# Where each tile's first expert weights come from: loads by SyncE into four slots in place of VectorE copies

## What is computed

```python
z = _layernorm(x, ln_g, ln_b)
logits = jnp.einsum('bth,he->bte', z, rW) + rb
probs = jax.nn.softmax(logits, axis=-1)
topv, topi = jax.lax.top_k(probs, TOP_K)
...
hid = jax.nn.gelu(jnp.einsum('bth,ehf->btef', z, W1) + b1, approximate=False)
outs = jnp.einsum('btef,efh->bteh', hid, W2) + b2
mixed = jnp.sum(outs * w[..., None], axis=2)
return x + mixed
```

## Time and profile before

| what | us |
|---|---|
| median of 3 runs (lowest, highest) | 833.07 (832.11, 835.7) |
| the profiled execution | 831.73 |
| its span in the trace | 829.9 |
| PE busy in it | 753.3 (91%) |
| DVE, ACT, POOL busy | 631.3, 563.3, 535.9 |
| granted TensorE clock, mean | 0.956 |

### The profile page before, as it was taken

One profiled execution on the slowest core, in us unless ns is written; L12 is line 12 of the kernel. 1 busy time (PEld: TensorE's weight loads), 2 busy tenths in 40 slices (PEclk: granted clock), 3 DMA queues, 4 the chain that ended last, 5 costly groups with the idle time before them and its releaser, 6 DMA issues.

```text
span 829.9 us, 26089 instructions
## 1 busy us (share of the span) xinstructions
PE 753.3 (91%) x8080; PEld 587.1 (71%) x8081; DVE 631.3 (76%) x1781; ACT 563.3 (68%) x1469; POOL 535.9 (65%) x609
## 2 busy tenths in 40 slices
PE   7888989999999999999999997666967898999995
PEld 4555666777777777777777665455867797999995
DVE  7788998988999999989999999963347763444442
ACT  3466777878888888878888874445464554666663
POOL 5433757777777767768767765354555556777773
PEclk9999999999999999999999999757989898999998
DMA  8566775777687786886786775551333333443432
GB/s 213 149 145 154 153 159 121 166 169 162 154 190 154 162 182 140 182 162 156 170 175 155 176 148 103 147 168 39 60 56 53 52 46 58 77 61 62 62 64 27
DMA packets 154004, 104.46 MB, mean 126 GB/s; under 512 B 68365, under 2 KB 149561, under 8 KB 153817
## 3 DMA queue, kind: packets, MB, share of 16 engines
q1 hardware_dynamic: 135502, 79.47, 43.7%
q0 software_dynamic: 10944, 14.10, 10.8%
q10 hardware_dynamic: 7498, 10.18, 4.2%
HBM read 36.65 MB, written 17.33 MB: 65 GB/s over the span
## 4 chain that ended last, share of the span: by engine, by line
PE 59%; DVE 13%; DMA 10%; POOL 5%; issue 5%; SPq 3%; ACT 2%; DVEq 1%; ACTq 0%; POOLq 0%
PE s_row L1021 9%; PE pj L916 8%; PE zt L962 7%; PE s_row L930 7%; PE s_t L950 7%; PE pj L883 7%; PE pj L1032 4%; PE zt L1032 4%; DVE negmax L1409 3%; DMA stack_x<-in_x 2%; DMA out_x<-index_space,idx_s 2%; PE pj L901 2%; SPq L672 2%; DMA stack_x<-k_part 2%; PE pj L1009 1%
## 5 line engine op out<-in xcount | busy, mean ns | idle before, releaser
L1409 DVE TENSOR_REDUCE negmax<-s_row 100x1 f32<-100x361 f32 x512 | 251.0, 522 | 20.0 <-PE s_row L930 16.0
L1226 ACT ACTIVATE p_t<-s_t 128x400 f32<-128x400 f32 x384 | 187.9, 499 | 89.7 <-PE s_t L950 82.1
L930 PE MATMUL s_row<-stack_x,q_stack 125*128 125x361 bf16 x512 | 134.0, 321 | 22.8 <-DVE negmax L1409 16.3
L744 POOL DMA_INDIRECT out_x<-index_space,idx_s x56 | 91.3, 1631 | 74.6 <-DMA out_x<-index_space,idx_s 27.8
L950 PE MATMUL s_t<-q_stack,stack_x 128*128 128x100 bf16 x1536 | 129.1, 212 | 8.8 <-ACT p_t L1226 6.1
L950 PEld LDWEIGHTS s_t<-q_stack,stack_x 128*128 128x128 bf16 x1536 | 94.6, 99 | 53.1 <-issue 25.0
L1021 PE MATMUL s_row<-w_qkv,v_aug 128*128 128x128 f32 x912 | 119.1, 288 | 8.2 <-DVE v_aug L1504 8.2
L1021 PEld LDWEIGHTS s_row<-w_qkv,v_aug 128*128 128x128 f32 x912 | 114.0, 204 | 9.5 <-DVE v_aug L1504 9.4
L1414 DVE TENSOR_SCALAR p_t<-p_t 128x1200 f32<-128x1200 f32 x128 | 100.8, 787 | 11.1 <-ACT p_t L1226 11.0
L916 PE MATMUL pj<-w_qkv,ct 128*128 128x256 f32 x384 | 104.9, 396 | 0.3 <-ACT k_rest L1147 0.3
L962 PE MATMUL zt<-p_t,v_aug 128*32 128x100 f32 (+1 forms) x3072 | 96.1, 260 | 0.0
(11 more groups left out here) (247 smaller groups left out, 1436.6 us busy)
## 6 DMA issues: line engine op xcount, KB each, us to landing
stack_x<-k_part SPq DMA_DIRECT2D x192, 192.0 KB, 3.6
q_stack<-q_part SPq DMA_DIRECT2D x192, 64.0 KB, 2.0
ct<-in_ctx_t SPq DMA_DIRECT2D x32, 361.0 KB, 4.4
stack_x<-in_w ACTq DMA_DIRECT2D x8, 512.0 KB, 6.2
w_s<-in_w ACTq DMA_DIRECT2D x14, 256.0 KB, 3.1
zscr<-zn SPq DMA_DIRECT2D x32, 100.0 KB
z_in<-zscr SPq DMA_DIRECT2D x32, 100.0 KB
zf_d<-zf_s SPq DMA_DIRECT2D x32, 100.0 KB
```

Source lines behind the costliest of these rows:

```text
L744: pool.indirect_dma_start(out_rows[0:n], bass.IndirectOffsetOnAxis(idx_out(k), 0), result_rows(k), None, bounds_check=n - 1, oob_is_err=Fa ...
L930: nc.tensor.matmul(s_row[h % 2][:, 0:KEYS], q_stack[0:MROW, b.slot, h, :], k_stack[0:MROW, b.slot, h, 0:KEYS], start=True, stop=True).then ...
L1226: nc.scalar.activation(p_t[:, quad % 2, kt, :], s_t[g % 2][:, 0:4 * Q], ACT.Exp).then_inc(exp_done, 1)
L1409: v.tensor_reduce(negmax[:, b.slot, h:h + 1], s_row[h % 2][0:Q, 0:KEYS], AXIS.X, ALU.max, negate=True).then_inc(max_done, 1)
```

## The change

The host packs each expert's first weights and bias into one DRAM block of 128 rows of 1028 floats (4112 bytes a row, 526 KB). `w1_s`, `b1_s`, their loads and the DVE step `weights` go. Four slots `w1_k` take their place; SP reads the expert of tile k+4 from `te_i`, waits until `gelu(k)` has read its slot, and loads the block. `up` waits for that DMA, `gelu` takes its bias from the slot. The first four loads stand at a place of their own ("w1", 375). `gating` gets a wait for `gated` of four tiles before. The places of routing, early tiles and the last three batches are all dealt anew; of these tables only a part is shown.

```diff
-        w1_s = sb(es, "w1_s", [128, 2, E, HF])
+        w1_k = sb(es, "w1_k", [128, 4, 2 * HF + 4])
...
-            w1_k = [v_aug[:, k].rearrange("p n w -> p (n w)")[:, 0:2 * HF] for k in (2, 0)]
...
-                    sp.dma_start(b1_s[:], b1).then_inc(b1_loaded, 16)
+
+                def load_w1(k):
+                    sp.wait_ge(tiles_known, 2 if k.known and k.index >= NF else 1)
+                    e = sp.value_load(te_i[0:1, bass.ds(k.index, 1)], min_val=0, max_val=E - 1)
+                    after(sp, gelu_done, 4 * (k.index - 3))
+                    sp.dma_start(w1_k[:, k.ring], w1[bass.ds(e, 1)].rearrange("e p f -> p (e f)")).then_inc(w1_copied[k.ring], 16)
+
+                def tile_step(k):
+                    if not k.known or k.index + 4 < NT:
+                        load_w1(k.later(4))
...
+                        if at("w1"):
+                            for c in range(4):
+                                load_w1(Tile(0, c))
+                        for k in tiles_at(turn, i, s):
+                            tile_step(k)
...
+                remaining(sp, tile_step, LOOP[0])
...
-                    pe.wait_ge(w1_copied, k.index + 1)
+                    pe.wait_ge(w1_copied[k.ring], 16 * k.turn + 16)
...
-                    act.wait_ge(b1_ready, k.index + 1)
...
-                                             bias=b1_k[:, k.slot, j:j + 1]).then_inc(gelu_done, 1)
+                                             bias=w1_k[:, k.ring, 2 * HF + j:2 * HF + j + 1]).then_inc(gelu_done, 1)
...
+                    after(dve, y_ready, k.index - 3)
...
-                def weights(k):
-                    e = dve.value_load(te_i[0:1, bass.ds(k.index, 1)], min_val=0, max_val=E - 1)
-                    after(dve, up_done, k.index - 1)
-                    v.tensor_scalar(w1_k[k.slot].rearrange("p (c f) -> p c f", c=2), w1_s[:, :, bass.ds(e, 1), :].rearrange("p c e f -> p c (e f)"),
-                                    1.0, None, ALU.mult).then_inc(w1_copied, 1)
...
-TILE_PLACE = [393, 393, 394, 396, 396, 400, 406, 406, 407, 410, 412, 412, 415, 415, 421, 425, 427, 438, 440, 442, 442, 446, 448, 451]
-WEIGHT_LOADS = (27, 30, 31)
+TILE_PLACE = [392, 393, 395, 395, 395, 398, 403, 406, 408, 409, 410, 411, 417, 417, 422, 422, 423, 423, 429, 434, 434, 435, 436, 439]
+WEIGHT_LOADS = (30, 31)
```

More of the change, by code:

```diff
@@ L155, in pipeline, with build @@
         iteration(0, i)
-def build(nc, x, ctx_t, wq_t, bq, wk_t, bk, wv_t, bv, gamma, beta, ln_g, ln_b, rw, rb, w1, b1, w2, b2,
+def build(nc, x, ctx_t, wq_t, bq, wk_t, bk, wv_t, bv, gamma, beta, ln_g, ln_b, rw, rb, w1, w2, b2,
           ident_d, route_c, zscr, zf_d, out):
@@ L182, in build @@
         lnb_c = sb(es, "lnb_c", [128, 2])
-        b1_s = sb(es, "b1_s", [128, E, 4])
-        route_const, rw_scaled, shift_done, rb_shifted, b1_loaded = (sem(k) for k in (
-            "route_const", "rw_scaled", "shift_done", "rb_shifted", "b1_loaded"))
+        route_const, rw_scaled, shift_done, rb_shifted = (sem(k) for k in ("route_const", "rw_scaled", "shift_done", "rb_shifted"))
         rb_s = sb(es, "rb_s", [Q, E])
-        w1_s = sb(es, "w1_s", [128, 2, E, HF])
+        w1_k = sb(es, "w1_k", [128, 4, 2 * HF + 4])
         ident = sb(es, "ident", [128, 128])
@@ L195, in build @@
         ident_ready = sem("ident_ready")
-        w1_loaded = sem("w1_loaded")
+        w1_copied = [sem(f"w1_copied{k}") for k in range(4)]
         x2_step = sem("x2_step")
@@ L558, in build @@
             gate = sb(att, "gate", [128, 4])
-            b1_k = sb(att, "b1_k", [128, 2, 4])
             idx_g_ready, idx_s_ready = sem("idx_g_ready"), sem("idx_s_ready")
@@ L562, in build @@
             scattered = [sem(f"scattered{k}") for k in range(2)]
-            zgt_done, zgt_copied, up_done, b1_ready, gelu_done = (sem(k) for k in ("zgt_done", "zgt_copied", "up_done", "b1_ready", "gelu_done"))
+            zgt_done, zgt_copied, up_done, gelu_done = (sem(k) for k in ("zgt_done", "zgt_copied", "up_done", "gelu_done"))
             gate_ready, y_biased, down_done, y_ready = (sem(k) for k in ("gate_ready", "y_biased", "down_done", "y_ready"))
-            w1_copied = sem("w1_copied")
             N_W2 = 16 * (E + 1)
@@ L1250, in iteration @@
                             queries_high(a)
[L1251 to L1255, removed]
                         n, g = lagging(turn, i, s, SCORES_LAG)
@@ L1521, in tile_step @@
                     if not k.known or k.index + 2 < NT:
-                        weights(k.later(2))
                         gating(k.later(2))
@@ L1531, in first_tiles @@
                     dve.wait_ge(w2_loaded, N_W2)
[L1532 to L1536, removed]
                     for c in range(2):
@@ L1675 @@
 PLACE = {"PE": PE_PLACE, "ACT": ACT_PLACE, "DVE": DVE_PLACE, "POOL": POOL_PLACE, "SP": SP_PLACE}
-ROUTE_PLACE = {"sum_const": 295, "ask0": 299, "exp0": 309, "prob0": 311, "choose00": 321, "choose01": 335, "sum0": 353, "ends0": 354, "places0": 357,
[6 rows of a table removed]
-TILE_PLACE = [393, 393, 394, 396, 396, 400, 406, 406, 407, 410, 412, 412, 415, 415, 421, 425, 427, 438, 440, 442, 442, 446, 448, 451]
-WEIGHT_LOADS = (27, 30, 31)
-TAIL = {29: {'PE': {'z': 8, 'zft': 2, 'router': 4}, 'ACT': {'td': 7, 'u': 6, 'y': 14, 'zft': 2, 'zt': 6}, 'DVE': {'z': 9, 'stats': 3, 'var': 4, 'stats2': 8, 'var2': 10, 'logits': 2}, 'POOL': {'u': 2, 'rstd': 2, 'xb': 7, 'y': 10, 'rstd2': 11}, 'SP': {'zout': 5, 'zin': 8, 'zf': -1}},
-        30: {'PE': {'z': 10, 'zft': -7, 'router': -6}, 'ACT': {'td': 12, 'u': 3, 'y': 5, 'zft': -6, 'zt': 4}, 'DVE': {'z': 7, 'stats': 0, 'var': 1, 'stats2': 3, 'var2': 4, 'logits': -6}, 'POOL': {'u': 1, 'rstd': 2, 'xb': 2, 'y': 4, 'rstd2': 5}, 'SP': {'zout': 5, 'zin': 11, 'zf': 0}},
-        31: {'PE': {'z': 9, 'zft': -6, 'router': -5}, 'ACT': {'td': 7, 'u': 4, 'y': 5, 'zft': -7, 'zt': 6}, 'DVE': {'z': 7, 'stats': 0, 'var': 3, 'stats2': 3, 'var2': 4, 'logits': -6}, 'POOL': {'u': 0, 'rstd': 1, 'xb': -3, 'y': 3, 'rstd2': 4}, 'SP': {'zout': 8, 'zin': 10, 'zf': -10}}}
@@ new lines @@
+ROUTE_PLACE = {"sum_const": 304, "ask0": 307, "exp0": 309, "prob0": 311, "choose00": 322, "choose01": 335, "sum0": 350, "ends0": 351, "places0": 357,
+               "taken0": 361, "split0": 368, "hot00": 369, "hot01": 370, "number00": 371, "number01": 373, "query00": 374, "query01": 374, "lanes00": 373,
+               "lanes01": 374, "lanes02": 375, "lanes03": 376, "gates0": 345, "store0": 348, "picks0": 378, "experts0": 377, "w1": 375, "index0": 379,
+               "gather": 380, "rows": 385, "affine": 383, "tiles": 386, "gelu": 386, "ask1": 402, "exp1": 400, "prob1": 405, "choose10": 406,
+               "choose11": 409, "sum1": 409, "gates1": 409, "store1": 417, "ends1": 411, "places1": 415, "taken1": 415, "split1": 418, "hot10": 419,
+               "hot11": 419, "hot12": 423, "hot13": 424, "query10": 418, "query11": 423, "query12": 423, "query13": 424, "lanes10": 423, "lanes11": 428,
+               "experts1": 429, "picks1": 434, "index1": 432}
@@ new lines @@
+TILE_PLACE = [392, 393, 395, 395, 395, 398, 403, 406, 408, 409, 410, 411, 417, 417, 422, 422, 423, 423, 429, 434, 434, 435, 436, 439]
+WEIGHT_LOADS = (30, 31)
+TAIL = {29: {'PE': {'z': 9, 'zft': 2, 'router': 3}, 'ACT': {'td': 9, 'u': 6, 'y': 14, 'zft': 4, 'zt': 7}, 'DVE': {'z': 9, 'stats': 3, 'var': 4, 'stats2': 10, 'var2': 11, 'logits': 3}, 'POOL': {'u': 1, 'rstd': 2, 'xb': 0, 'y': 4, 'rstd2': 10}, 'SP': {'zout': 6, 'zin': 9, 'zf': 1}},
+        30: {'PE': {'z': 7, 'zft': -8, 'router': -6}, 'ACT': {'td': 12, 'u': 3, 'y': 5, 'zft': -6, 'zt': 7}, 'DVE': {'z': 7, 'stats': 0, 'var': 1, 'stats2': 3, 'var2': 4, 'logits': -5}, 'POOL': {'u': 2, 'rstd': 2, 'xb': 2, 'y': 3, 'rstd2': 6}, 'SP': {'zout': 4, 'zin': 12, 'zf': -4}},
+        31: {'PE': {'z': 7, 'zft': -9, 'router': -6}, 'ACT': {'td': 8, 'u': 2, 'y': 4, 'zft': -8, 'zt': 7}, 'DVE': {'z': 8, 'stats': -1, 'var': 0, 'stats2': 1, 'var2': 3, 'logits': -7}, 'POOL': {'u': -1, 'rstd': 1, 'xb': -3, 'y': 2, 'rstd2': 2}, 'SP': {'zout': 6, 'zin': 7, 'zf': -11}}}
```

8 lines of the change are left out of this document (2 added, 6 removed), and 6 rows, old and new, of the table ROUTE_PLACE.

## The result

The changed kernel takes 852.47 us (median of 4 runs, 851.41 to 853.22) against 832.99: **1.0225 times as long, 95% interval 1.0194 to 1.0256**. The forecast was 825.6 in a range of 812 to 843.

A forecast was written before the change was run, and what follows sets the result against it. PE was taken as full in attention and late tiles, with gains only between about 552 and 690, where it waits; -8.0 - 5.0 + 5.5 = -7.5 gave 824.2 us profiled, 825.6 median, range 812 to 843.

The forecast's parts named there:

- The copy: Last batches to early tiles: without DVE's copy of first weights, PE's waits and the slow clock behind them go; 8.0 us won.
- the late routing: Dealt anew between tile steps: one more DVE stretch holding a result up, 1.6 us taken off the copy's gain.
- The loads: 57 loads of 526 KB, one per tile, fit the DMA engines but delay scatters and gathers: 5.5 us lost.
- L: What the loads add to the landing of a scatter or gather: 0.75 us, between 0 and 2.3.
- the slack of 0.63 a group: Late tiles: POOL's 14.33 us beside PE's 14.96 per four-tile group leaves 0.63 us for L; eight groups cost 1.0.
- The first gathers: First gather, beside the first four loads, and tile 24's gather: each later by L, together 1.5 us.
- The new places: Last batches and early tiles: tile 5 ahead of batch 31's rows wins 3.7 us, an earlier wait 1.3; together 5.0.
- At nothing: Costed at zero: removed ACT issues, SP's new waits for expert list and gelu, DVE's gate wait, the loads' cover.
- The cover of the loads: Each load, issued at tile k's gelu and wanted by `up(k+4)`, has 3 us to spare.
- The rival: Scatters become the bound: POOL waits for landings at expert changes, then DVE; at L = 2.0, 843 us; chance 0.18.
- The signs: If right: copy waits gone, scatter landing about 4.5 us instead of 3.8, late tiles at 3.74 to 3.8 us each.
- early loads: Early tiles: eight scatters waiting for the landing before them, 8 x 0.75 = 6, half counted: 3.0 us lost.

The follow-up runs named there:

- e5: Changed kernel with the old places, and from the fifth tile on loads of the bias alone, first weights left out: 830.4 us, ratio 0.9974.
- e4: Changed kernel, every wait and place kept, but from the fifth tile on a load brings only the bias: 833.7 us, ratio 0.9991.
- e1: Control: changed kernel with POOL's scatter wait count loaded with stated bounds, as in all further variants: 852.0 us, ratio 1.0201.
- e3: Loads alone: changed kernel with the old tables of places, full loads of 526 KB a tile: 846.0 us, ratio 1.0143.
- e11: e3 with full loads for the early tiles alone; tiles from the 25th on load only the bias: 835.4 us, ratio 1.0007.
- e8: e4 with the old places of the tiles, but the new places of routing and last batches: 839.0 us, ratio 1.0076.
- e9: Changed kernel with DVE's writing of the routing's constants back at place 295 instead of 304: 848.0 us, ratio 1.0168.
- e12: e3 with the same bytes in rows of 512 B instead of 4112 B, bias by its own small load: 849.8 us, ratio 1.0192.
- e6: Changed kernel, but from tile 28 on a load waits for the up product two tiles back, not gelu four back: 851.6 us, ratio 1.0239.

## Why the prediction was wrong

- **The copy, -8.0: right in its place, not in the total.** Between tiles 7 and 23 the early tiles are 7.2 us shorter without copies (79.7 to 72.5, e5), and a wait for gelu of 1.4 us took the place that was given 1.5. The 2.4 us at the late routing, where 1.6 was given, lie inside this. Lost again are 3.1 us at tile 0 and 1 us elsewhere, so that 3 us are left by the profiles and 2 by the ratios.
- **The loads, +5.5: the step that failed.** They cost 0.021 of the time, 17.5 us, in the new places (e4 to e1) and 0.0169, 14 us, in the old ones (e5 to e3). Of these 14 the early tiles have some 3 (e11), hardly parted from nothing but the size of their term; the late tiles have some 11 where the sum had 8 x (0.75 - 0.63) = 1.0. Two sizes in that term were wrong. L was set at 0.75; the median landing rose by 0.6 to 0.9, near that, but what counts are landings that POOL waits for, and there a scatter came 6.04 us after the one before instead of 4.55, 1.5 us more; the first of all 8.11 instead of 4.77. And the slack of 0.63 a group was worked out for groups of four tiles. The group from 785.60 to 798.16 has three scatters: with 4.55 + 2 x 3.26 = 11.07 beside PE's 3 x 3.74 = 11.22 it had 0.15. It took 12.56, 1.3 beyond PE. POOL's waits for landings in the late stretch are 25.2 us where they were 15.4, 9.8 more, and PE lost 9.7 (125.8 to 135.5).
- **The first gathers**, put at L, cost more. With the same places the first one landed after 5.7 us (e3) instead of 3.1, L = 2.6, and tile 0 came 2.3 us later (558.7 to 561.0). First the gather of e3, then that of the kernel before:

```profile
DMA to landing us min/median/max: 5.7/5.7/5.7
```

```profile
DMA to landing us min/median/max: 3.1/3.1/3.1
```

- **The new places, -5.0: the wrong sign.** That tiles go ahead of the last batch's rows is worth something, some 7 us (e8). But the rows were taken to come "no sooner", and no later was assumed with it, "behind the same four scatters", and these came later: rstd at 612.34 instead of 599.53. Of these 12.8 us the first scatter was already 10.2 late (593.86 instead of 583.66), as tile 0 was 9.7 (568.4 instead of 558.7); the scatters themselves added 2.6. PE's wait moved behind tiles 5 and 6 and grew:

```profile
620.27 0.59 PE L987 MATMUL tr<-ident,zf_s 100*128 100x100 f32 x2 [8.61 <-ACT zf_s L1183]
```

  The routing's places were costed at nothing, and one of them alone, the constants, costs some 3 us (e9). From e3 to e1 the places cost 0.0058, 5 us. The traces show one more place ahead of tile 0: in all seven kernels with the new places of routing and last batches PE waits 5.1 to 6.1 us for a transfer of the last batch into `q_stack`, and in all seven with the old ones 0.6 to 1.6. SP's list has that transfer behind `z_in`, which waits for a store to land (`zscr`). First SP and PE in the kernel before, then in the changed one:

```profile
535.42 0.29 SPq L657 DMA_DIRECT2D zscr<-zn  x1
...
538.72 0.28 SPq L651 DMA_DIRECT2D z_in<-zscr  x1
539.38 0.76 SPq L654 DMA_DIRECT2D q_stack<-m_part  x1
...
545.12 0.52 PE L950 MATMUL s_t<-q_stack,stack_x 128*128 128x100 bf16 x4 [1.11 <-DMA q_stack<-m_part]
```

```profile
539.51 0.29 SPq L661 DMA_DIRECT2D zscr<-zn  x1
...
545.45 0.28 SPq L655 DMA_DIRECT2D z_in<-zscr  x1
545.77 0.76 SPq L658 DMA_DIRECT2D q_stack<-m_part  x1
...
551.09 0.52 PE L960 MATMUL s_t<-q_stack,stack_x 128*128 128x100 bf16 x4 [5.13 <-DMA q_stack<-m_part]
```

  What it carries, `m_part`, was ready at 539.36 and at 540.12. In the new places the store is issued 0.4 us ahead of three 512 KB loads of ACT's queue (539.88), and `z_in` comes 5.9 us behind it instead of 3.3. That this costs tile 0 some 4 us is read from the traces; no run undid it alone. Which of the remaining numbers of routing and last batches are to blame was not tried.
- **At nothing:** right for SP's and DVE's new waits, as far as e4 shows, which has all of them and the time of the kernel before. The cover of the loads held in the changed kernel: no wait of PE for a load is shown.
- **The rival** that came true for the loads is the one on the other side, in its place and with its sign. POOL's waits for landings grew as said, and DVE's, the second half of it, from 33.0 to 83.0 us in the late tiles; but PE waited there for gathers alone and for no result. It had 0.18 and 843 us, with L = 2.0 and 23.0 us for the loads, more than they cost; the time came out 10 us above it because the two gains that it took as safe were, for the most part, not there.
- **The signs.** "Scatter landing at about 4.5 us" stood for a right forecast and came true, at 4.4, beside a wrong time; the late tiles took 4.1 us each (135.5 for 33), not 3.74 to 3.8. The median hides the landings that somebody waits for.

By the ratios, from the kernel before to the changed one: copies away and four loads -2 us (e5), early bytes +3 (e11), late bytes +11 (e3), new places +5 (e1), together +17, as e1 itself has it (1.0201); the changed kernel's own runs had 19.5. In the terms of the sum: late loads 1.0 given, 11 found; new places -5.0 given, +5 found; copy and first gathers -6.5 given, -2 found; early loads 3.0 given, 3 found.

## What to carry to other kernels

A transfer that "fits" by its share of the DMA engines can still cost: ask how late the transfers it meets will land, those with a wait on them and not the median one, and how much slack the engine has that waits for them, in its shortest group and not in the mean one. A resident table with a copy on an idle engine is cheap where DMAs with waits on them share the time; a wait for such a copy is worth no more than the next wait behind it. And an operation that is moved to another place is not free of what runs beside it there.

## What the runs showed of the hardware

The price of a load beside scatters is not proportional to its bytes here: at shares of 0.41, 0.61 and 0.80 of the DMA engines the late tiles took 126.0, 126.1 and 134.1 us. Neither rows of 512 B instead of 4112 (e12) nor another moment (e6) made it less.

A DVE operation of 0.45 us took 2.15 beside GpSimd. POOL's timeline beside it:

```profile
439.87 1.18 POOL L831 TENSOR_TENSOR u<-z_in,td 100x256 f32<-100x256 f32 x1 [0.51 <-DMA z_in<-zscr]
...
441.01 1.56 POOL L822 TENSOR_TENSOR k_part<-k_rest,k_part 128x722 bf16<-128x722 f32 x1
```

DVE started at 440.49, inside the first of these, and ended at 442.64; POOL's second ended at 442.57. The Trainium skill ("SBUF — State Buffer", section "SBUF: two separate sides") says that a DVE operation in a mode with two ports (or one with two inputs in SBUF, against a GpSimd operation that reads SBUF) shares one pair of ports with GpSimd, and that whichever starts first holds it for the whole instruction while the other is fully blocked. The rows agree that DVE is blocked and not slowed in proportion: it ends with POOL, 0.07 us behind. They do not show DVE's mode, and POOL's second operation, begun 0.52 us after DVE's, went ahead of it too, which that rule alone does not give. DVE ended with POOL in the kernel before, at 428.08, beside an operation of POOL that is over at 428.01; only that one takes 0.73 us and not 1.56:

```profile
427.28 0.73 POOL L787 TENSOR_TENSOR xb<-stack_x,row_c 100x256 f32<-100x256 f32 x1
```
